# Narrow-head attention with queries and keys cleared first and score products over all 32 rows of a row group

## What is computed

```
scores = jnp.einsum('bhqd,bhkd->bhqk', q, k) * SCALE
scores = jnp.where(causal[None, None], scores, -jnp.inf)
probs = jax.nn.softmax(scores, axis=-1)
ctx = jnp.einsum('bhqk,bhkd->bhqd', probs, v)
```

## Time and profile before

| | |
|---|---|
| median of 3 runs | 2746.41 us (2738.42 to 2749.94) |
| profiled execution | 2746.3 us, span 2744.5 us |
| mean granted TensorE clock | 0.803 |
| TensorE busy (products) | 2074.4 us, 76% |
| VectorE busy | 1602.8 us, 58% |
| ScalarE busy | 787.7 us, 29% |
| GpSimd busy | 570.8 us, 21% |
| chain that ended last | TensorE 55%, VectorE 34%, ScalarE 4% |
| first pass of layer 0 | about 48 to 90 us of the span |
| second pass of layer 0 | about 93 to 154 us |
| first pass of layer 6 | about 915 to 1005 us |
| second pass of layer 6 | about 1010 to 1130 us |

### The profile page before, as it was taken

One profiled execution on the slowest core, in us unless ns is written; L12 is line 12 of the kernel. 1 busy time (PEld: TensorE's weight loads), 2 busy tenths in 40 slices (PEclk: granted clock), 3 DMA queues, 4 the chain that ended last, 5 costly groups with the idle time before them and its releaser, 6 DMA issues.

```text
span 2744.5 us, 27737 instructions
## 1 busy us (share of the span) xinstructions
PE 2074.4 (76%) x9734; PEld 1308.8 (48%) x9734; DVE 1602.8 (58%) x2454; ACT 787.7 (29%) x1999; POOL 570.8 (21%) x325
## 2 busy tenths in 40 slices
PE   6774659746636888788888974454799999999986
PEld 3541234412213446566666743333566675555843
DVE  3259965879977441445555339999366514444214
ACT  1233311233312014355555211111255403444010
POOL 1212530005410003233333115655100000000010
PEclk9566879658867655689999986776799999999966
DMA  3000011010010210000001010000000100000000
GB/s 99 6 32 0 0 15 37 5 48 0 0 39 3 32 41 1 1 20 11 11 11 54 1 69 0 0 0 0 4 10 10 43 8 12 11 11 20 1 31 16
DMA packets 25727, 48.98 MB, mean 18 GB/s; under 512 B 6262, under 2 KB 19603, under 8 KB 24092
## 3 DMA queue, kind: packets, MB, share of 16 engines
q1 hardware_dynamic: 25644, 47.85, 5.8%
HBM read 42.20 MB, written 1.05 MB: 16 GB/s over the span
## 4 chain that ended last, share of the span: by engine, by line
PE 55%; DVE 34%; ACT 4%; issue 4%; SPq 1%; POOL 1%; DMA 1%; DVEq 0%; ACTq 0%; POOLq 0%
DVE big L789 7%; PE banks L1110 7%; PE banks L1079 7%; PE banks L1119 6%; PE banks L1048 6%; DVE big L1790 5%; PE banks L1102 3%; PE banks L414 3%; DVE big L1786 3%; PE banks L389 3%; PE banks L425 2%; PE banks L1344 2%; PE banks L386 2%; DVE big L784 2%; DVE big L770 1%
## 5 line engine op out<-in xcount | busy, mean ns | idle before, releaser
L1185 DVE COPY arena<-banks 128x512 f32<-128x512 f32 x196 | 135.5, 691 | 329.4 <-PE banks L1102 326.3
L218 POOL TENSOR_TENSOR ln_rstd<-ln_var_eps,neg_half 128x2 f32<-128x2 f32 x48 | 36.9, 768 | 1065.5 <-DVE ln_var_eps L206 1065.5
L1079 PE MATMUL banks<-big 128*128 128x256 f32 x784 | 235.7, 413 | 6.0 <-ACT big L1221 4.4
L1110 PE MATMUL banks<-arena,big 128*128 128x256 f32 x784 | 227.7, 414 | 6.3 <-DVE arena L1185 6.3
L1242 ACT ACTIVATE arena<-banks,arena 128x256 f32<-128x256 f32 x392 | 193.4, 500 | 61.0 <-DVE arena L1159 43.1
L789 DVE TENSOR_TENSOR_SCAN big<-big 128x2048 f32<-128x2048 f32 x32 | 203.4, 6355 | 1.1
L701 PE MATMUL banks<-big,ident 128*128 128x512 f32 x288 | 171.3, 750 | 38.1 <-POOL big L862 38.1
L862 POOL TENSOR_TENSOR big<-big 128x2048 f32<-128x2048 f32 x32 | 144.8, 4525 | 251.7 <-DVE big L789 251.7
L1048 PE MATMUL banks<-x_feat,arena 128*128 128x512 f32 x392 | 176.3, 592 | 0.0
L1119 PE MATMUL banks<-arena,big 128*128 128x256 f32 x784 | 174.3, 382 | 1.9 <-ACT big L1260 1.9
L1260 ACT ACTIVATE big<-banks 128x256 f32 (+1 forms) x196 | 75.3, 384 | 347.9 <-PE banks L1110 347.9
(11 more groups left out here) (311 smaller groups left out, 3706.7 us busy)
## 6 DMA issues: line engine op xcount, KB each, us to landing
big<-big SPq DMA_DIRECT2D x32, 64.0 KB, 2.3
arena<-in_L0f_w SPq DMA_DIRECT2D x1, 2048.0 KB, 8.1
arena<-in_L1a_wo SPq DMA_DIRECT2D x1, 2048.0 KB
arena<-in_L1f_gv SPq DMA_DIRECT2D x1, 2048.0 KB
arena<-in_L2a_qk_w SPq DMA_DIRECT2D x1, 2048.0 KB
big<-big SPq DMA_DIRECT2D x64, 32.0 KB
arena<-in_L2x_wo SPq DMA_DIRECT2D x1, 2048.0 KB
arena<-in_L2x_q_w SPq DMA_DIRECT2D x16, 128.0 KB, 2.0
```

The costliest lines, as they stand in the source:

```text
L1079: last = mm(ps[:, h * SEQ:(h + 1) * SEQ], q[:, b * SEQ + h * P:b * SEQ + (h + 1) * P], k[:, b * SEQ:(b + 1) * SEQ], start=True, stop=not s ...
L1110: last = mm(slot, self.v[:, 2 * b + kc, :], self.probs_t[:, u % 2, kc, :], start=(kc == 0), stop=(kc == 1))
L1185: v.tensor_copy(self.probs_t[:, u % 2].rearrange("p a b -> p (a b)"), B[4 + u % 2][:]).then_inc(self.turn_read, 1)
```

## The change

q is filled with 0.0 on GpSimd ahead of its fill of v, and k is filled with 0.0 on VectorE behind the packing of weights. SyncE waits for the fill of k before the ones, and for that of q before the moves. The ones count in the semaphore of the first half of the moves (`moved[0]`), no longer with the maxima (`rows_moved`). Both score products contract over all 32 rows of a row group. In the first pass row w is then part of the product: it holds ones in k and zero in q, because the maxima of a group are put there only after its first pass.

```diff
+        self.k_cleared = s(name + "_k_cleared")
...
         e.wait_x_feat(sp, l)
         sp.wait_ge(e.consts_made, 1)
+        sp.wait_ge(self.k_cleared, 1)
         for j in range(4):
             row = 32 * j + w
-            sp.dma_start(self.k[row:row + 1].rearrange("o g t -> o (g t)"), e.ones[0:TILES * self.groups, :]).then_inc(self.rows_moved, 16)
+            sp.dma_start(self.k[row:row + 1].rearrange("o g t -> o (g t)"), e.ones[0:TILES * self.groups, :]).then_inc(self.moved[0], 16)
         for blk in range(2):
             for s in range(2):
                 sp.wait_ge(self.staged, 4 * blk + 2 * s + 2)
+                sp.wait_ge(self.cleared, 1)
...
-    def rows(self, j, more=0):
-        return slice(32 * j, 32 * j + self.width + more)
+    def rows(self, j):
+        return slice(32 * j, 32 * j + 32)
...
-                pe.wait_ge(self.moved[g // self.per_block], 16 * 8 * self.per_block)
+                pe.wait_ge(self.moved[g // self.per_block], 16 * (8 * self.per_block + 4 * (g == 0)))
...
             if u == 0:
-                pe.wait_ge(self.rows_moved, 16 * 4 * (G + 1))
+                pe.wait_ge(self.rows_moved, 16 * 4 * G)
...
-                    rows = self.rows(j, 1)
+                    rows = self.rows(j)
...
         dve.sem_inc(self.prepared, 1)
-        dve.wait_ge(self.cleared, 1)
+        e.wait_x_feat(dve, self.l)
+        nc.vector.memset(self.k, 0.0).then_inc(self.k_cleared, 1)
+        dve.wait_ge(self.cleared, 2)
...
         e.wait_x_feat(pool, self.l)
+        nc.gpsimd.memset(self.q, 0.0).then_inc(self.cleared, 1)
         nc.gpsimd.memset(self.v, 1.0).then_inc(self.cleared, 1)
```

## The result

| | before | after |
|---|---|---|
| median | 2743.4 us (4 runs, 2738.4 to 2749.9) | 2666.8 us (4 runs, 2661.7 to 2669.1) |
| profiled execution | 2746.3, span 2744.5 | 2666.5, span 2664.5 |
| mean granted clock | 0.803 | 0.844 |

The ratio is 0.9717 (95% interval 0.969 to 0.9744): 2.8% faster. The forecast was 2662. New are 478 (VectorE fills k) and 579 (GpSimd fills q); the fill of v, 574, is 580.

What follows compares the result with a forecast made beforehand. TensorE at granted clock 0.50 was taken to set the first pass and stand in the second's loop. First passes -34.5, second passes -50, transposes -2.2, later start +2.7 made -84 from 2746.3: 2662 us, range 2644 to 2724.

Steps and rivals of the forecast that it cites:

- Rival C: Both passes: rows within a row group don't matter to the clock, only the later start is left; 2749 us, chance 0.10.
- Forecast -9.5 and -25.0: First passes of layers 0 and 6: four units go from 11.1 to 7.65 us at full clock; sum 34.5 us saved.
- 39 units at 1.28: Second passes: 12 units in layer 0 and 27 in layer 6 each save 1.28 us at full clock, 50 us.
- I take a rise 15 us into each layer's pass: Second passes: clock assumed to reach 1.00 after 15 us, chosen between at once and never; 50 us saved.
- rivals A and B: Clock rises in first passes only (2714.5 us, 0.26), or in one second pass, or late (2679 or 2698 us, 0.18).
- my immediate rise: Bound of the forecast: clock up at once everywhere, 46 second-pass units saving 1.28 us each, 59 us; 2651 us in all.
- Rival A: Clock rises in the first passes only; the second pass keeps its gaps and 3.73 us per unit; 2714.5 us, chance 0.26.
- Forecast +2.7: Layer 6's start: SyncE's ones and moves wait for the fill of k, shifting everything by 2.7 us.
- by that slope 8192 elements take 6.9 us: Layer 6's start: VectorE's fill of k priced from the difference between its 256- and 24-element fills, 6.9 us.
- Both start at 885.4: Layer 6's start: VectorE's fill of k and GpSimd's of q begin together at 885.4 us; ones go out at 892.3.
- the longer fill: Layer 6's start: alternative price for VectorE's fill of k from the 256-element fill alone, 8.7 us.
- rival D: Layer 6's start: the two fills collide, moves start 9.7 us later, the clock does nothing; 2756 us, chance 0.04.

Runs made afterwards that it cites:

- Clears only: The changed kernel with clears and waits kept but row counts set back to 16 and 8, 17 and 9: 2749.8 us, 1.0019 to before.
- first only: The changed kernel with 32 rows in the first pass alone, the second contracting over 17 and 9: 2717.0 us, 0.9898 to before.
- 24 rows with filler: The fastest kernel (k filled with ones, unread 128-row products ahead of passes) with 24 instead of 32 rows in both passes: 2711.2 us, 0.9855 to before.
- second only: The changed kernel with 32 rows in the second pass alone, the first contracting over 16 and 8: 2692.9 us, 0.9819 to before.
- delayed kernel: The changed kernel with ScalarE copying the last group's maxima five times instead of once, so second passes begin later: 2668.7 us, 0.9696 to before.
- Ones filled in: The changed kernel with k filled with ones instead of zeros, without the DMAs of ones; q's moves wait for q's fill alone: 2662.6 us, 0.9672.

## Why the prediction was right, and where it was off

**The mechanism** was read rightly from the earlier trace rows: what holds the clock at 0.50 in these passes is the count of rows fed, and busy time alone doesn't decide. Clears only and first only differ in nothing but rows, and in layer 6's first pass TensorE is busy for 94% of the time at 0.50 with 8 rows and for 78% at 1.00 with 32. The Trainium skill, "TensorE: Matmul & The Clock Gate", section "What's actually happening", lets the gate follow how busy TensorE has been and names no rows; this pair disagrees. Gaps matter beside the rows, as the 24 rows with filler and the late rises with 32 show. Rival C, that rows within a row group don't matter, falls with the same pair, and its premise of equal product lengths is true all the same: 1.66 us for 8 and for 24 rows.

**First passes.** Forecast -9.5 and -25.0, measured -9.5 and -25.9. Layer 6 needed two units for the rise where I took three. That layer 0 came out to the tenth is luck: the kernel before lost 1.00 after 10 us in the profile that I priced from, but with the same 16 rows three other kernels kept it for 22 to 26 us and took 33.1 to 36.1 us, against which 31.4 us is a gain of 1.7 to 4.7.

**Second passes.** Forecast 39 units at 1.28, -50; measured -44.9. The step that was off is "I take a rise 15 us into each layer's pass": it came after 21 and 32 us. The loop itself was better than my price, 2.38 for 2.45, and paid part of that back. Forecast and rivals A and B treated the delay as a property of the kernel; second only (3 us) and the delayed kernel (40 and 21) show that it isn't, and ten passes had 3 to 40 us. So it is luck as well that a guess of 15 us for both layers came within 5 us of the measured total: with a rise 3 us into both passes, as in second only, the same kernel would have come out some 16 us lower (41.1 + 79.2 in place of 47.2 + 89.4). With the passes entered at 1.00 the term is 20.4 + 42.2 = 62.6, near the 59 of my immediate rise plus its 3 us for the shorter loop. Rival A had expected that 1.00 never comes in a pass with a quarter of idle time; it comes in every second pass with 32 rows, ten of ten.

**Layer 6's start.** Forecast +2.7, measured +4.6. GpSimd's fill was priced right, 6.92 us for 7.0, but the step "by that slope 8192 elements take 6.9 us", with "Both start at 885.4", failed for VectorE. Its row is 6.88 us long, but it begins 1.76 us behind x, so from x to its end VectorE takes 8.64 us: the 8.7 of the longer fill (272 ns for 256 elements), which I had put aside. With 8.7 my own sum gives 4.3 us instead of 2.7. Layer 0 says the same: its fill ends at 28.56, where the longer price had 28.6 and the slope 27.7. Whether VectorE idles ahead of its row or the row begins late, no run here tells. Ones filled in shows that the term was the fill of k and the DMAs of ones ahead of the moves. The two fills didn't slow each other: from the end of its last copy VectorE takes 4.5 us for 4096 elements in layer 0, where GpSimd is no longer filling, and from x 8.64 for 8192 beside GpSimd, whose own rows go from 3.51 to 6.92. This is what the Trainium skill's "SBUF — State Buffer", section "Who interferes with whom", has for a VectorE instruction with at most one SBUF input, and the 9.7 us of rival D are gone. Layer 0: forecast 0; the ones end and the first move starts at 31.27, where the earlier trace rows have 31.65. The transposes gave 1.1 us each, as forecast.

## What to carry to other kernels

Where TensorE is the bound at a granted clock of 0.50 though it is hardly idle, look at the rows of its products: zeros in the unused rows of a row group lengthened no product here and took the clock from 0.50 to 1.00. In a stretch with many gaps the rise may be tens of microseconds late; products that nobody reads, over all rows, in the wait just ahead of it made it begin at 1.00, but in that stretch only 32 rows of each group kept it there, not 24. When the moment at which the clock turns differs between profiles, compare lengths of passes, not totals: layers that nobody touched moved by 13 us between two profiles here.

## What the runs showed of the hardware that was not expected

- The moment of a rise moved by 19 and 11 us when its pass was shifted by 1.2 us, while two executions of one kernel agreed to 0.2 us. The moment of a fall moved too: 10 and 22 us into layer 0's first pass in two kernels that are the same up to its end but for filler just ahead of the last turned maximum.
- 1.00 is kept with less than it takes to reach it: 24 rows in layer 6's first pass stay at 0.50 for 89 us when it begins there and at 1.00 for 61 us when it begins there.
- The row of VectorE's fill of 8192 elements starts 1.7 to 1.8 us behind its last condition in every profile of layer 6, that of 4096 elements 1.03 us behind the last copy in layer 0, while GpSimd's starts at once. Lag and row together are 8.64 and 4.5 us, 1.05 and 1.10 ns per element, near the 1.06 of the 256-element fill; the rows alone have 0.84 and 0.85. Price such a fill from its condition to its end.
